# A routed feed-forward layer: result rows added into the output by scatters, and one addition from DRAM to DRAM at the end

## What is computed

```python
xf = _layernorm(x)                                  # 2048 tokens x 128
logits = xf @ Wg                                    # 16 experts
_, topi = jax.lax.top_k(logits, 2)                  # two experts for each token
gates = softmax over the two chosen logits
for e in range(16):
    h = jax.nn.silu(xf @ W1[e] + b1[e]) * (xf @ W11[e] + b11[e])
    y = y + (h @ W2[e] + b2[e]) * gates[:, e, None]
z = jax.nn.silu(xf @ Ws1 + bs1) * (xf @ Ws11 + bs11) @ Ws2 + bs2    # shared expert
out = x + y + z
```

## Time and profile before

| | us |
|---|---|
| median of 3 runs | 338.8 (338.71 to 342.55) |
| time of the profiled execution | 339.4 |
| its span, first to last instruction | 337.6 |
| mean granted TensorE clock | 0.979 |

### The profile page before, as it was taken

How to read it: one execution, slowest core, us unless ns; L and a number is a source line. 1 busy time by engine, 2 the same in 40 slices (tenths; PEclk the granted TensorE clock), 3 DMA queues, 4 the chain that set the end, 5 groups by cost and what they waited for, 6 DMA issues and landing times.

```text
span 337.6 us, 6077 instructions
## 1 busy us (share of the span) xinstructions
PE 281.9 (84%) x1869; PEld 207.5 (61%) x1869; DVE 215.7 (64%) x712; ACT 161.9 (48%) x317; POOL 124.4 (37%) x203
## 2 busy tenths in 40 slices
PE   0138799899999899998998988988899999999900
PEld 0026455465656456565564556877789999999900
DVE  7976945575574777758677368864445565555606
ACT  1413555555595454954558556452344544544400
POOL 0324023223311332565318300537106666666630
PEclk9999999999999999999999999999999999999965
DMA  7999500000000000000000100114616858484237
GB/s 267 344 374 398 238 2 0 1 2 2 2 0 0 2 0 3 25 26 8 8 2 33 34 0 1 34 34 123 193 32 175 254 151 249 139 248 132 74 109 289
DMA packets 21759, 33.80 MB, mean 100 GB/s; under 512 B 2672, under 2 KB 11600, under 8 KB 21600
## 3 DMA queue, kind: packets, MB, share of 16 engines
q1 hardware_dynamic: 19200, 28.20, 26.3%
q0 software_dynamic: 2528, 5.22, 4.5%
HBM read 23.95 MB, written 9.45 MB: 99 GB/s over the span
## 4 chain that ended last, share of the span: by engine, by line
PE 66%; DVE 18%; ACT 5%; issue 4%; DMA 4%; SPq 1%; POOL 1%; POOLq 0%; DVEq 0%; ACTq 0%
PE ps L1383 7%; PE ps L1365 6%; DVE mpad L576 6%; PE ps L1371 6%; PE ps L1295 5%; PE ps L1109 4%; PE ps L1138 4%; PE ps L1152 4%; PE ps L1069 4%; PE ps L1070 4%; PE ps L1071 4%; PE ps L1110 3%; PE ps L1148 3%; PE ps L1122 3%; PE ps L1136 3%
## 5 line engine op out<-in xcount | busy, mean ns | idle before, releaser
L576 DVE TENSOR_REDUCE mpad<-ps 128x2 f32<-128x308 f32 x128 | 55.3, 472 | 36.4 <-PE ps L1110 36.0
L818 POOL TENSOR_SCALAR ks<-k_stack,cst 128x160 fp32r<-128x160 f32 x64 | 30.0, 483 | 100.1 <-DVE k_stack L561 100.1
L890 POOL DMA_INDIRECT result_rows<-yo,dest x47 | 45.1, 960 | 41.4 <-DVE yo L792 41.1
L955 ACT ACTIVATE pf<-ps 128x512 f32<-128x512 f32 x80 | 46.5, 597 | 18.2 <-PE ps L1152 10.2
L1110 PE MATMUL ps<-ks,qs 96*128 96x308 f32 x128 | 46.2, 416 | 0.0
L856 POOL DMA_INDIRECT slot_rows<-xr,slot x32 | 31.3, 979 | 37.3 <-DVE slot L483 28.8
L1109 PE MATMUL ps<-mq_b,identb 128*128 128x308 bf16 x128 | 38.8, 308 | 4.8 <-DVE mpad L576 3.8
L1138 PE MATMUL ps<-qs,ks 128*128 128x512 f32 x64 | 37.1, 581 | 0.0
L1109 PEld LDWEIGHTS ps<-mq_b,identb 128*128 128x128 bf16 x128 | 12.5, 98 | 33.0 <-issue 26.3
L783 DVE SCALAR_TENSOR_TENSOR e_h<-ps,wu,e_s 128x128 f32<-128x128 f32 x62 | 19.0, 347 | 20.0 <-PE ps L1371 19.9
L1056 ACT ACTIVATE e_s<-ps,wu 128x128 f32<-128x128 f32 x62 | 19.4, 364 | 25.1 <-PE ps L1365 25.1
(11 more groups left out here) (203 smaller groups left out, 628.5 us busy)
## 6 DMA issues: line engine op xcount, KB each, us to landing
wu<-w_up SPq DMA_DIRECT2D x31, 258.0 KB, 3.3
wr<-w_up SPq DMA_DIRECT2D x1, 4128.0 KB, 22.2
slot_rows<-zero SPq DMA_DIRECT2D x1, 3120.0 KB, 24.5
xg<-slot_rows SPq DMA_DIRECT2D x12, 260.0 KB, 3.4
wd<-w_down SPq DMA_DIRECT2D x1, 2048.0 KB, 12.1
xo<-result_rows SPq DMA_DIRECT2D x4, 512.0 KB, 5.4
xs<-x SPq DMA_DIRECT2D x1, 1024.0 KB, 4.8
out<-xs SPq DMA_DIRECT2D x4, 256.0 KB, 2.3
```

The lines of the kernel that those rows point to most:

```text
L576: dve.tensor_reduce(mpad[:, m % 2, q, 96 + 2 * a:98 + 2 * a], ps[:, KS_ + a, 0:2 * SK].rearrange("p (c k) -> p c k", c=2), AX.X, ALU.max, ...
L890: pool.indirect_dma_start(out=result_dram[:, :], out_offset=bass.IndirectOffsetOnAxis(ap=dest[:, n:n + 1], axis=0), in_=yo[:, n % 4, :], i ...
L955: act.activation(pf[:, n % RP, :], ps[:, ST_ + n % 2, :], ACT.Exp, scale=DK ** -0.5).then_inc(exp_done, 1)
```

## The change

The output tensor becomes one DRAM tensor of three regions of rows: SPARE = 512 spare rows, then 2048 rows (first region), then 2048 rows (second region). The host takes the first region as the result. `result_dram`, `xo`, the loads back and DVE's eight additions are gone. SP fills the spare rows and the second region with zeros after the fill of `slot_dram`, and stores each final piece of `xs` into the first region (`store_first`), two pieces before it waits for `sent` and two after the first two `load_rows`. The tokens' first expert rows are added into the first region and the second ones into the second region by the scatters themselves, with `compute_op=ALU.add`; POOL first waits for all the fills and stores (`primed`). The spare rows are shared by tiles of the same place in their groups. After all scatters have landed, POOL issues one DMA that adds the second region to the first, DRAM to DRAM.

```diff
+SPARE = 4 * P
...
-        result_dram = nc.dram_tensor("result_rows", (SLOTS + 2 * TOK, D), F32, kind="Internal").ap()
...
-        xo = sb("xo", [P, NT, 2, D])
...
+        first_rows = out[SPARE:SPARE + TOK, :].rearrange("(p t) d -> p t d", p=P)
+        second_rows = out[SPARE + TOK:SPARE + 2 * TOK, :].rearrange("(p t) d -> p (t d)", p=P)
...
+            sp.dma_start(out[0:SPARE, :].rearrange("(p a) d -> p (a d)", p=P), zero[:, 0:4 * D]).then_inc(primed, 16)
+            sp.dma_start(second_rows, zero[:, 0:NT // 2 * D].unsqueeze(1).to_broadcast([P, 2, NT // 2 * D])
+                         ).then_inc(primed, 16)
...
+            def store_first(c):
+
+                sp.wait_ge(x2_done, c + 1)
+                sp.dma_start(first_rows[:, QT * c:QT * c + QT, :], xs[:, QT * c:QT * c + QT, :]).then_inc(primed, 16)
...
             sp.wait_ge(tile_known, 1)
             for d in range(RW):
                 load_weights(d)
+            for c in range(2):
+                store_first(c)
             sp.wait_ge(sent, 2 * NT * 16)
             for g in range(2):
                 load_rows(g)
+            for c in range(2, B):
+                store_first(c)
...
-            for r in range(4):
-                sp.wait_ge(returned[r], (RUN - r + 3) // 4 * 16)
-            pairs = result_dram[SLOTS:SLOTS + 2 * TOK, :].rearrange("(p t k) d -> p t k d", t=NT, k=2)
-            for c in range(B):
-                sp.dma_start(xo[:, QT * c:QT * c + QT, :, :], pairs[:, QT * c:QT * c + QT, :, :]).then_inc(ld_r[c], 16)
-            for c in range(B):
-                sp.wait_ge(out_done, c + 1)
-                sp.dma_start(out[:, QT * c:QT * c + QT, :], xs[:, QT * c:QT * c + QT, :]).then_inc(stored, 16)
             sp.wait_ge(zeroed, 16)
-            sp.wait_ge(stored, 16 * B)
+            sp.wait_ge(primed, 16 * (2 + B))
+            sp.wait_ge(stored, 16)
...
-            for c in range(B):
-                dve.wait_ge(ld_r[c], 16)
-                rows = xs[:, QT * c:QT * c + QT, :]
-                link(dve.tensor_tensor(rows, rows, xo[:, QT * c:QT * c + QT, 0, :], ALU.add))
-                dve.tensor_tensor(rows, rows, xo[:, QT * c:QT * c + QT, 1, :], ALU.add).then_inc(out_done, 1)
...
+            pool.wait_ge(primed, 16 * (2 + B))
             for n in range(RUN):
                 pool.wait_ge(yo_done, n + 1)
-                pool.indirect_dma_start(out=result_dram[:, :],
+                pool.indirect_dma_start(out=out[:, :],
                                         out_offset=bass.IndirectOffsetOnAxis(ap=dest[:, n:n + 1], axis=0),
-                                        in_=yo[:, n % 4, :], in_offset=None).then_inc(returned[n % 4], 16)
+                                        in_=yo[:, n % 4, :], in_offset=None, compute_op=ALU.add
+                                        ).then_inc(returned[n % 4], 16)
+            for r in range(4):
+                pool.wait_ge(returned[r], (RUN - r + 3) // 4 * 16)
+            pool.dma_start(out[SPARE:SPARE + TOK, :].rearrange("(p t) d -> p (t d)", p=P),
+                           out[SPARE + TOK:SPARE + 2 * TOK, :].rearrange("(p t) d -> p (t d)", p=P),
+                           accum_op=ALU.add, max_dma_last_dim=4096).then_inc(stored, 16)
```

More of the change, by code:

```diff
@@ L59 @@
 C_SPARE = C_TILE + TILES
-C_DEST = C_SPARE + TILES
+C_DEST = C_SPARE + 4
 C_QUAD = C_DEST + 2 * NT
@@ L238, in build @@
          x2_done, tx_mm, xgt_done, meta_done, gate_mm, lin_mm, esilu_done, eh_done,
-         ey_mm, yo_done, out_done, stored, ld_d) = (sem(n) for n in (
+         ey_mm, yo_done, stored, primed, ld_d) = (sem(n) for n in (
             "ld_x ld_c ld_w ld_m ld_ctx ld_b zeroed dve_step cleared scanned "
@@ L246, in build @@
             "silu_done h_done w2_mm x2_done tx_mm xgt_done meta_done "
-            "gate_mm lin_mm esilu_done eh_done ey_mm yo_done out_done stored ld_d").split())
+            "gate_mm lin_mm esilu_done eh_done ey_mm yo_done  stored primed ld_d").split())
         ld_f = [sem(f"ld_f{par}") for par in range(2)]
@@ L250, in build @@
         ld_u = [sem(f"ld_u{r}") for r in range(RW)]
-        ld_r = [sem(f"ld_r{c}") for c in range(B)]
         returned = [sem(f"returned{r}") for r in range(4)]
@@ L772, in meta @@
                 dve.tensor_tensor(dest[:, cols].unsqueeze(2), xg[:, g % 2, :, D + 1:D + 2],
-                                  cst[:, C_SPARE + 4 * g:C_SPARE + 4 * g + 4].unsqueeze(2),
+                                  cst[:, C_SPARE:C_SPARE + 4].unsqueeze(2),
                                   ALU.max).then_inc(meta_done, 1)
@@ L1425, in constants @@
     c[:, C_TILE:C_TILE + TILES] = np.arange(TILES)
-    c[:, C_SPARE:C_SPARE + TILES] = P * np.arange(TILES) + p[:, None]
+    c[:, C_SPARE:C_SPARE + 4] = P * np.arange(4) + p[:, None]
     for k in range(2):
-        c[:, C_DEST + NT * k:C_DEST + NT * k + NT] = SLOTS + 2 * (NT * p[:, None] + np.arange(NT)) + k
+        c[:, C_DEST + NT * k:C_DEST + NT * k + NT] = SPARE + TOK * k + NT * p[:, None] + np.arange(NT)
     for r in range(3):
@@ L1494 @@
            for name, a in arrays.items()]
-    out = nc.dram_tensor("out", (P, NT, D), F32, kind="ExternalOutput").ap()
+    out = nc.dram_tensor("out", (SPARE + 2 * TOK, D), F32, kind="ExternalOutput").ap()
     build(nc, *aps, out)
     r = run_bass_kernel_spmd(nc, [arrays], core_ids=[0])
-    return r.results[0]["out"].transpose(1, 0, 2).reshape(B, S, D)
+    rows = r.results[0]["out"][SPARE:SPARE + TOK].reshape(P, NT, D)
+    return rows.transpose(1, 0, 2).reshape(B, S, D)
```

## The result

| | before | after |
|---|---|---|
| median (4 runs each) | 338.75 us (338.18 to 342.55) | 359.94 us (358.46 to 360.56) |
| span of the profiled execution | 337.6 | 356.6 |
| granted TensorE clock | 0.979 | 0.968 |

The ratio is 1.059, with a 95% interval from 1.051 to 1.068: slower by 6%, where 0.7% faster was forecast. A few executions of a kernel are slower at a lower granted clock; ratios and intervals rest on the others, and so are not exactly those of the medians. The span grew by 19.0 us.

The account below looks back on a forecast made before the run. TensorE, busy 60 of 60 us, bounds the routed stage; only the 12.3 us ending can be won. 325.3 + 0.7 + 0.1 + 8.8 + 0.2 = 335.1 us span, given as 336.5 median; range 332.4 to 353.

Parts of the forecast that it names:

- I take at most 0.1 more, since 0.96 us for 128 rows need not be by the row, and cost it at nothing: Routed stage: POOL's time per adding scatter grows at most 0.1 us from 0.96, hidden by TensorE's pace, costing nothing.
- The condition that stood beside it: Routed stage: POOL's scatter instruction may grow from 0.96 to 1.25 us before POOL paces the stage.
- rival 2: Routed stage: POOL's adding scatter exceeds 1.25 us and paces; 343.5 us at 1.4, 367.5 at 1.92; chance 0.09.
- the last landing: Start of the ending: the addition's read of its destination moves the last scatter's landing from 325.3 to 326.0, 0.7 us.
- the ending: After the last scatter lands: 12.3 us of loads, additions and stores replaced by 0.1 waits, 8.8 addition, 0.2 end.
- the sum: Whole kernel: 325.3 + 0.7 + 0.1 + 8.8 + 0.2 = 335.1 us span, 2.5 us less than before.
- rival 1: Routed stage: adding scatters land later than 5.6 us, so yo's four buffers pace; 353 us at 7 us; chance 0.15.
- The fills and stores: SP's queue around the start of the routed stage: new fills and stores stay hidden and cost nothing.
- The new wait on `primed` costs nothing: Before POOL's first scatter at 252.46: the last store lands at about 249.7, 250.7 at worst, so no delay.
- the forecast's world: Routed stage: TensorE stays busy throughout and sets the pace at 1.56 us per tile, hiding POOL's scatters.
- The estimate that I made from its figures: Final addition: 4.2 us at 15.5 GB/s per engine plus 2.26 us of a small scatter, 6.5 us; not used.
- the 8.8 from the loads back: Final addition: 8.2 us, as the old ending's 2 MB of loads took, plus 0.6 us for POOL's descriptors.

## Why the prediction was wrong

**The step that failed** is "I take at most 0.1 more, since 0.96 us for 128 rows need not be by the row, and cost it at nothing". The reason given was true, but a part that is not by the row can grow too: the addition costs 0.60 us, of which some 0.42 are fixed, six times what I allowed. The condition that stood beside it was right: POOL paces from 1.25 us on, and 1.56 + 0.30 = 1.86 against 1.56 for 46 intervals gives 14 us; 15.3 were measured, since the 46 intervals before were 1.534 on the mean, not 1.56. This is rival 2, to which I gave 0.09. Its two prices (343.5 at 1.4 us, 367.5 at 1.92) enclose the result, but partly by luck: at the measured 1.56 us its own formula gives 336.5 + 46 x 0.30 = 350.3. Of the 23.4 us between 336.5 and 359.9, 15.3 are POOL's pace, 3.1 the later first scatter, 0.2 the last landing, 2.9 the ending, and 1.9 the distance of the median from the profiled span (3.3 us here, 1.4 in the sum), mostly because the profiled execution was the fastest of the four. With only 0.3 us of room per tile, 47 times, and no row for the adding form, its price had to be in the range up to the upper end; I cut the range at 353, where rival 1 was priced.

**Rival 1** had more weight and was wrong: landings went to 4.5 in the median and 5.2 at most, where I had put 3.8 and 5.6, and twice the buffers changed nothing.

**The fills and stores** cost TensorE nothing, as forecast: the first turn starts at 246.67 against 246.41, and the weights' issue before it was already 0.3 us later (231.70 against 231.43). The stores took 4.0 us to land in the median, not 2.3, but had all landed at 250.1. "The new wait on `primed` costs nothing" was wrong: the first scatter starts 3.1 us later, 0.3 of it because its rows were later (ready at 252.44 against 252.18), and 2.9 because it starts 3.15 us behind its rows instead of 0.28. I looked at when the semaphore is met, and not at what the wait instruction does to the engine that holds it. In the forecast's world POOL would have made this up, as it does in the run with plain scatters; where POOL paces, it counts in full.

**The ending**: sized at 0.1 + 8.8 + 0.2 = 9.1 us behind the last landing, measured 12.0. The addition itself was put too high (8.8, measured 7.7), POOL's way to issue it too low (0.1, measured 0.7), and the end too low by 3.3 us, POOL's drain, for which the sum had no term. The row was there in the trace before, a drain that ended at 321.6 + 8.9 = 330.5, hidden under the loads back:

```profile
L126 POOLq DRAIN  x1: 8895/8895/8895, 321.6 to 321.6; - x1
```

Together this is 2.9 us more than the sum, and of the 3.2 us to be won 0.3 are left; the run with plain scatters (340.4 against 339.7) says the same: had POOL's price been nothing, the change would have made no difference.

The Trainium skill ("Collectives: The Full Stack", section "The bandwidth ceiling: the fold count and why AG ≠ RS ≠ AR") says that the price of an add in the DMA's path is its second read. The runs show the addition 2.8 us dearer than the copy of the same size, which fits; that it is the second read no run shows. The estimate that I made from its figures, 6.5 us, was 1.2 us below the measured 7.7; the 8.8 from the loads back was 1.1 above it.

## What to carry to other kernels

An edit that adds a mode to an instruction issued once per tile is priced first on the engine that issues it: compare the room per tile (here 0.3 us) with the whole possible growth, and let the range reach there. When a ring of buffers shows waits for landings, look at whether the issuing engine ever waits; if the gap between two of its instructions is always the shortest (here 0.30 us), more buffers won't help. And a transfer moved to POOL at the very end brings POOL's drain with it; rows that are final early can be fetched early instead, which is what won 1.3% here, on one chip.

## What the runs showed of the hardware that was not expected

- A scatter of 128 rows of 512 B occupies POOL 0.96 us plain and 1.56 with addition; with 64 rows 0.91 and 1.42. In all cases 0.30 us go between two when POOL has work waiting.
- With addition the software queue counts 144 packets for each scatter ((7792 - 32 x 32) / 47, in the run with SP's copy) instead of 32 (2528 / 79).
- POOL's drain at the end of the block ends 3.3 us behind the landing of a direct DMA that POOL issued, in every run that ends with one, addition or copy, and 5.2 us behind a scatter's (330.5 against 325.3 in the kernel before), or 5.2 us from its own start where that came after the landing (344.2 to 349.4, with SP's copy). A last DMA by SP has 0.5 us behind it.
- With an added wait on POOL, long met or not, the scatter behind it started 1.1 us behind its rows in one kernel and 3.0 to 3.2 in another, instead of 0.3.
- 1 MB from DRAM to DRAM took 4.9 to 5.2 us as a copy and 7.7 to 8.8 us as an addition.
